# A two-layer macaron block on one core: in the dense stages PE turns the next chunk's norm ahead of the down projection of the preceding chunk

## What is computed

```
x = x + 0.5 * ffn0(norm(x))     # dense, stage 1
x = x + mix(norm(x))            # time mixing with a decaying scan, stage 2
x = x + 0.5 * ffn0(norm(x))     # dense, stage 3
x = x + 0.5 * ffn1(norm(x))     # eight experts, top 2, stage 4
x = x + flow(norm(x))           # causal flow attention, stage 5
x = x + 0.5 * ffn1(norm(x))     # stage 6

def ffn0(x):                    # w_* are integers times 1/127
    gate = x @ w_gate.T         # 128 -> 384
    up = x @ w_up.T             # 128 -> 384
    return (silu(gate) * up) @ w_down.T   # 384 -> 128
```

## Time and profile before

| | |
|---|---|
| median of 3 runs | 1009.77 us |
| the three runs | 1008.24, 1009.77, 1009.98 us |
| the profiled execution's own time | 1007.76 us |
| its span, first to last instruction | 1006.0 us |
| PE busy | 859.9 us (85%) |
| DVE busy | 711.1 us (71%) |
| ACT busy | 638.6 us (63%) |
| POOL busy | 604.4 us (60%) |
| mean granted clock of PE | 0.947 of full speed |

### The profile page before, as it was taken

One profiled execution on the slowest core, in us unless ns is written; L12 is line 12 of the kernel. 1 busy time (PEld: TensorE's weight loads), 2 busy tenths in 40 slices (PEclk: granted clock), 3 DMA queues, 4 the chain that ended last, 5 costly groups with the idle time before them and its releaser, 6 DMA issues.

```text
span 1006.0 us, 14102 instructions
## 1 busy us (share of the span) xinstructions
PE 859.9 (85%) x3862; PEld 460.3 (46%) x3862; DVE 711.1 (71%) x1535; ACT 638.6 (63%) x1153; POOL 604.4 (60%) x610
## 2 busy tenths in 40 slices
PE   7879677767975999999996688888886899999997
PEld 6734333354432444444443355555543344444443
DVE  6945469965563878887863277777786787887774
ACT  3167489967755887778783444444322787778884
POOL 2064675667458766666675254444457766667674
PEclk9999788869997999999997799999997999999999
DMA  8000000000002222211120000000000213223320
GB/s 213 11 1 0 0 0 1 1 1 1 1 0 85 84 86 85 79 48 58 69 84 0 1 1 0 1 1 1 1 1 1 101 69 95 94 94 95 94 95 22
DMA packets 27406, 42.10 MB, mean 42 GB/s; under 512 B 5320, under 2 KB 19036, under 8 KB 27356
## 3 DMA queue, kind: packets, MB, share of 16 engines
q1 hardware_dynamic: 27356, 41.52, 13.0%
HBM read 39.15 MB, written 2.36 MB: 41 GB/s over the span
## 4 chain that ended last, share of the span: by engine, by line
PE 35%; issue 22%; DVE 19%; POOL 14%; ACT 9%; SPq 1%; DVEq 0%; POOLq 0%; DMA 0%; ACTq 0%
PE bank L1478 7%; PE bank L1480 7%; PE bank L1479 7%; POOL arena L810 5%; POOL arena L754 4%; PE bank L1708 3%; DVE arena L1324 3%; ACT bank L1001 3%; POOL rstd L712 2%; DVE arena L1367 1%; DVE arena L1366 1%; DVE stats L1173 1%; PE bank L1678 1%; ACT arena L993 1%; PE bank L1715 1%
## 5 line engine op out<-in xcount | busy, mean ns | idle before, releaser
L790 POOL TENSOR_TENSOR arena<-arena 128x512 f16<-128x512 f32 x256 | 295.3, 1166 | 125.3 <-ACT arena L993 123.5
L1324 DVE TENSOR_TENSOR arena<-bank,arena 128x512 f32<-128x512 f32 x256 | 172.5, 685 | 79.6 <-ACT bank L1001 63.3
L993 ACT ACTIVATE arena<-arena 128x512 f16<-128x512 f32 x256 | 160.8, 628 | 73.8 <-DVE arena L1324 73.7
L1001 ACT ACTIVATE bank<-bank,eb 128x512 f32<-128x512 f32 x256 | 166.8, 656 | 18.9 <-PE bank L1480 18.5
L817 POOL TENSOR_TENSOR arena<-arena 128x512 f32<-128x512 f32 (+1 forms) x24 | 32.7, 1371 | 117.2 <-DVE arena L1442 89.9
L1478 PE MATMUL bank<-arena,ew1hi 128*128 128x512 f16 x256 | 98.5, 385 | 2.0 <-DVE arena L1324 2.0
L1479 PE MATMUL bank<-arena,ew1hi 128*128 128x512 f16 x256 | 98.5, 385 | 0.0
L1480 PE MATMUL bank<-arena,ew1lo 128*128 128x512 f16 x256 | 97.9, 382 | 0.0
L1478 PE MATMUL bank<-arena,ew2hi 128*128 128x512 f16 x256 | 97.3, 380 | 0.1
L1479 PE MATMUL bank<-arena,ew2hi 128*128 128x512 f16 x256 | 97.3, 380 | 0.0
L1480 PE MATMUL bank<-arena,ew2lo 128*128 128x512 f16 x256 | 97.3, 380 | 0.0
(11 more groups left out here) (274 smaller groups left out, 1876.2 us busy)
## 6 DMA issues: line engine op xcount, KB each, us to landing
arena<-wrows SPq DMA_DIRECT2D x64, 512.0 KB, 5.4
X<-in_L_attn_x_dram SPq DMA_DIRECT2D x8, 256.0 KB, 4.3
out_dram<-X SPq DMA_DIRECT2D x8, 256.0 KB, 6.7
arena<-in_L_ffn_ew_dram SPq DMA_DIRECT2D x2, 512.0 KB, 6.4
arena<-in_L_ffn_ew_dram SPq DMA_DIRECT2D x1, 1024.0 KB
wrows<-arena SPq DMA_DIRECT2D x16, 16.0 KB
arena<-in_L_ffn_gens_dram SPq DMA_DIRECT2D x1, 192.0 KB, 2.7
arena<-in_L_ffn_w_gate_dram SPq DMA_DIRECT2D x1, 192.0 KB, 2.9
```

What stands on the lines that cost most here:

```text
L790: pool.tensor_tensor(mo.hlo[:, u % 8, :], mo.hw[:, u % 4, :], mo.hhi[:, u % 8, :], ALU.subtract).then_inc(S.hlo, 1)
L993: A(mo.hhi[:, u % 8, :], mo.hw[:, u % 4, :], ACT.Copy).then_inc(S.hhi, 1)
L1001: A(bank[MM1_BANK[u]][:, :], bank[MM1_BANK[u]][:, :], ACT.Gelu, scale=1.0 / WS, bias=eb1[:, u:u + 1]).then_inc(S.gelu, 1)
L1324: TT(mo.hw[:, u % 4, :], bank[MM1_BANK[u]][:, :], mo.wB[:, p, u // EB, :], ALU.mult)\
```

## The change

In PE's step the two lines that turn the next chunk's norm move ahead of the down projection of the preceding chunk. Both stay between block 1 and block 2 of gate and up. Waits, increments, banks and all other engines' programs are as they were.

```diff
@@ -1574,6 +1574,8 @@
                                 last = three(dst[:, :], f0hi[:, k, cols], f0lo[:, k, cols], f0.xhi[:, p, :],
                                              f0.xlo[:, p, :])
                             last.then_inc(S.gu, 1)
+                        if lead and j == 1:
+                            turn_chunk(Z, 1 - p, S.z, i + 2, S.tr)
                         if lag and j == 1:
                             pe.wait_ge(S.hlo, HB * i)
                             for m in range(HB):
@@ -1582,8 +1584,6 @@
                                 last = three(bank[5][:, :], f0hi[:, 2, w], f0lo[:, 2, w], f0.hhi[:, u, :],
                                              f0.hlo[:, u, :], start=(m == 0), stop=(m == HB - 1))
                             last.then_inc(S.down_mm, 1)
-                        if lead and j == 1:
-                            turn_chunk(Z, 1 - p, S.z, i + 2, S.tr)
                     if lag:
                         pe.wait_ge(S.y, i)
                         after(pe, S.x, i - 1 + CREDIT)
```

## The result

The changed kernel takes 1020.25 us (median of 6 runs, 1019.23 to 1023.07) against 1009.38 us before (6 runs, 1008.23 to 1010.87): ratio 1.0113, 95% interval 1.0098 to 1.0127, so 10 to 13 us slower. The profiled execution has a span of 1018.0 us, 12.0 more than before.

What follows compares the result with a forecast made beforehand. The bound was a ring of hand-overs among four engines, none full, 7.41 us a step. Ten steps of +0.77 plus edges of 0.80 and 0.55 gave +9.0 on the median 1009.77: 1018.8 us, range 1014.5 to 1022.5.

Steps and rivals of the forecast that it cites:

- the sum: Added-up hand-over times of a dense-stage step and its edges; 4.65 us for stage one, 4.40 for two, together +9.0.
- the walk: Following one dense-stage step hand-over by hand-over through the engines' timelines; gave period 7.41 before and 8.22 after.
- one fall of the clock: Rival: PE drops to 1.2 GHz for one step, 1022.6 us; 6% together with a lasting fall, some 1064 us.
- The period before: Dense-stage step of the old kernel: a ring of hand-overs through POOL L754, no engine full, 7.41 us.
- The turn starts later, the gap grows: On PE, the turn put in front would start 0.53 later than the old down projection; gaps grow from 0.70 to about 1.5.
- D: The moment in a step when the down projection ends; other times in the step are counted from it.
- The new ring: Changed step: down projection, y copy, L925, L1229, block 0, silu 0, norm, turn, no longer POOL; period 8.22, +0.82.
- the one direct row: Single profile row where PE waited for L1229: block 0 starts 0.84 after L1229 starts; averaged with 0.75, giving +0.77 a step.
- The edges: First and last chunks of the dense stages: chunk 1 costs +0.80 in stage one, +0.55 in two; chunk 7 gives nothing back.
- the turn fills the gap: Rival: norm ready before PE's gap, by 83.1, so 0.44 comes off each of 12 steps, 1004.5 us; 3%.
- the delay is hidden: Rival: turn and down projection become ready together, the y path has slack, and they merely trade: 1008 to 1011 us; 4%.
- ACT's queue sets the new period: Rival: silu 0 held by ACT's queue at D+3.38, +0.54 to +0.65 a step, 1016.6 us; 25%.

Runs made afterwards that it cites:

- experiment 5: Kernel before, turn still behind the down projection, its one wait for three low halves split so each block waits for its own: 998.97 us, ratio 0.9891.
- experiment 1: Kernel before, with PE's wait for the next chunk's norm put ahead of the down projection and no work moved: 1016.3 us, ratio 1.0061.
- experiment 2: Changed kernel, with ACT's copy of the turned norm (L925) put ahead of the y copy (L936): 1018.04 us, ratio 1.0073.
- experiment 6: Changed kernel, turn ahead, with the down projection's one wait for three low halves split by block: 1017.57 us, ratio 1.0077.
- experiment 3: Changed kernel, with the turn ahead in the first dense stage only and the old order in the second: 1015.71 us, ratio 1.0051.

## Why the prediction was right

The prediction said 1018.8 us, 1014.5 to 1022.5, slower. Measured 1020.25, in the range, 1.5 above the point; against its own before, +10.9 where the sum had +9.0.

The mechanism is right, and the total owes something to a wide range. The period of +0.86 lies just outside the forecast's own +0.65 to +0.85 (62%), and the top that the walk gave by itself was 1019.6, 0.65 under the measured time. The range reached 1022.5 by an allowance for one fall of the clock, and none happened in the changed steps. So the sign and the ring are understood, while the total's place in the range is in part luck.

**The period before, 7.41 by the walk.** Right, and more strongly supported by experiment 5: with the wait for the last low half out of the way the period drops to PE's own work.

**The turn starts later, the gap grows.** Right. The walk had the turn 0.53 later than the old down projection; the wait alone (experiment 1) costs 7.94-7.41 = 0.53 a step, and the gap ahead of the turn is 1.09 where the sum had 1.07.

**The early turn buys nothing, because the y copy stands in front of L925.** Right: L925 at D+0.70 (89.14 against 88.44), 0.69 in the sum; experiment 2 takes the y copy out of the way and gains 0.28 a step.

**The new ring.** All its members are where the walk put them. With D = 88.44 the sum had L1229 at D+1.32, block 0 at D+2.16, silu 0 at D+3.66, the norm at D+4.13, the turn at D+5.83. The trace has 1.32, 2.15, and one step earlier (D = 80.17, silu 0 at 83.83, norm at 84.32, turn at 86.01) 3.66, 4.15, 5.84.

**The size: the term that was mis-sized** is the period, +0.77 taken and +0.86 measured (8.27). Two terms make the difference. The hand-over behind L1229 is the full 0.83 (89.76 to 90.59), so the one direct row was right and averaging it with the neighbour POOL's was wrong: 0.05. And the turn takes 0.49 when PE starts it out of a wait (86.01 to 86.50), 0.44 in the rows before, where it followed matmuls without a pause: 0.05. The walk's own period, 8.22 before averaging, plus this is the measured 8.27. Ten steps make 0.9 us.

**The edges.** From the stage's first matmul (46.79 before, 45.87 after) to the down projection of chunk 7 (105.76 in the earlier trace rows, 110.00 after) the first stage is 5.16 longer, 4.65 in the sum. In the second, from block 0 of chunk 1 (241.38 in the earlier trace rows, 247.11 after) to chunk 7 (289.03, 299.58) it is 4.82 longer, 4.40 in the sum. Nothing was given back in chunk 7, as forecast. Together 9.98, inside the interval of 9.9 to 12.8 that the ratio gives.

**What is left of the profiled 12.0**, about 2.0, lies outside the changed steps. It is the sum of four pieces: 0.92 less ahead of the first stage's first matmul, 0.33 less between the stages (105.76 to 235.39 before, 110.00 to 239.30 after), 1.82 more in one step, 1.45 more from 289.03 and 299.58 to the end. Only the 1.82 was followed up. It is a step at the low clock: block 0 of chunk 0 to block 0 of chunk 1 in the second dense stage took 5.99 before (235.39 to 241.38) and 7.81 after. The windows of this step, before, after and in experiment 6, then PE's timeline in the changed kernel:

```profile
235.39:241.38 5.99, 4.72 (x23) 2.07 (x23) 2.08 (x3) 4.38 (x10) 4.67 (x9) 1.00 0.00 0
239.30:247.11 7.81, 7.34 (x22) 3.01 (x23) 2.08 (x3) 4.62 (x10) 3.89 (x9) 0.63 0.00 0
241.63:247.61 5.98, 4.71 (x22) 2.06 (x23) 2.08 (x3) 4.37 (x10) 4.72 (x9) 1.00 0.00 0
```

```profile
239.30 0.61 PE L1478 MATMUL bank<-arena,f0hi 128*128 128x512 f16 x1 [1.54 <-DVE arena L1240]
...
244.40 0.95 PE L1561 MATMUL bank<-ident,Z 128*128 128x128 f32 x4
...
247.11 0.39 PE L1478 MATMUL bank<-arena,f0hi 128*128 128x512 f16 x1 [0.47 <-DVE arena L1229]
```

The matmul at 239.30 takes 0.61 where one at full clock takes 0.39. The step is not touched by the change in what it does; the clock stood differently when it came. Nor does the low clock follow the order of the turn: experiment 6, with the turn ahead in both stages, has the step at 1.00, and experiment 3, with the old order in this stage, has it at 0.62 and 7.81 long. What sets the clock there stays open. Whether the medians hold such a share too stays open as well: 10.9 less 9.98 is under the spread of the runs.

**TensorE's clock in the changed steps.** No fall: PE's gaps of 1.09 and 0.42 in each 8.27 us leave the granted clock at 1.00 (one step is shown above, and the windows view has 1.00 from 60 to 108 us, where PE is busy 40.74 of 48.00). The rule of the Trainium skill ("Perfetto Trace Analysis", section Matmul Optimizations) that matmuls should run back to back in batches, because the engine scales its power with utilization, did not decide here; the trace shows no loss to it in the steps with all three parts.

The prediction let the clock stand because of one gap of 1.78. It left out a longer one in the same stage of the kernel before: 3.51 idle ahead of 53.05, with a granted clock of 0.54 from 54 to 56. In the changed kernel the same gap is 3.52, and the clock stays at 1.00. So a gap's length alone did not tell, and the forecast for the clock was borne out more than it was shown. Its price for a fall was also too high: it took the longer matmul (634 against 379 ns) for the spacing, which goes from 0.22 to 0.43 (53.96 to 54.39 before), so 15 matmuls would be 3.2 a step and not 3.8.

**What was wrong in the signs to look for.** I expected the chain of waits to leave L754. It did not, in the changed kernel, though PE has not one wait for POOL in these steps; it did in experiment 6, with the same period. The waits list and the timelines were right from the start, the chain view was not evidence either way. The rivals: "the turn fills the gap" fell with the gap of 0.93 ahead of L1561; "the delay is hidden" with the period; "ACT's queue sets the new period" is what experiments 1 and 2 made of it (7.94 and 7.99, 7.94 in the sum), not the changed kernel.

## What to carry to other kernels

Ahead of swapping two pieces of work on an in-order engine, compare when each one's input is ready, not how long it takes: the piece with the later input put first holds up the ready one, and its result may still have to wait in the consumer's queue. Walk the whole ring from hand-over to hand-over, since a swap changes which engines are in it; a hand-over for which there is a direct row is taken at that row. Where a gap is one wait for several results, try splitting the wait before reordering: here it gave 10.6 us where the reordering lost 10.9.

## What the runs showed of the hardware that was not expected

- The four 128x128 transposes of L1561 took 0.49 us to the start of the next matmul out of a wait and 0.44 behind running matmuls (86.01 to 86.50 against 85.50 to 85.94 in the earlier trace rows).
- A hand-over to a waiting PE took 0.05 to 0.15 us past the end of the instruction it waited for: 0.06 behind POOL's L754 (83.49 to 83.55), 0.14 and 0.15 behind DVE's L1229 (89.76+0.69 = 90.45 to 90.59; 240.54+0.69 = 241.23 to 241.38 in the earlier trace rows), and 0.05 behind DVE's L1240, the same operation at the head of the second dense stage (234.65+0.69 = 235.34 to 235.39 before). Why L1229 and L1240 differ was not tried.
